# Exponent and high half head by head, low half of head 1 in the next pair, residual as float32 transposes scaled on GpSimd

## The reference

```python
xn = rms_norm(x, g_norm) * (1.0 + scale) + shift        # scale, shift from cond @ W_emb + b_emb
q, k, v = split_heads(xn @ W_qkv)                       # 16 heads of 64
q, k = rms_norm(q, g_q), rms_norm(k, g_k)
attn = softmax(q @ k.T * 64 ** -0.5)
o = attn @ v
x = x + (o + o @ W_out)
x = x + (conv(x, w) + b)                                # depthwise, four taps, causal
```

## Time and profile before

| | |
|---|---|
| median of 3 runs (lowest, highest) | 2456.92 us (2450.82, 2458.89) |
| profiled execution: its own time | 2456.85 us |
| its span on the core | 2454.9 us |
| TensorE matmul / VectorE / ScalarE / GpSimd busy | 95% / 84% / 73% / 26% |
| DMA queue 1, share of 16 engines | 93.4% |
| chain that ended last, by engine | PE 72%, DVE 11%, SyncE's queue 4%, issue 3% |

### The profile page before, as it was taken

One profiled execution on the slowest core, in us unless ns is written; L12 is line 12 of the kernel. 1 busy time (PEld: TensorE's weight loads), 2 busy tenths in 40 slices (PEclk: granted clock), 3 DMA queues, 4 the chain that ended last, 5 costly groups with the idle time before them and its releaser, 6 DMA issues.

```text
span 2454.9 us, 53605 instructions
## 1 busy us (share of the span) xinstructions
PE 2337.2 (95%) x20666; PEld 1529.3 (62%) x20666; DVE 2061.2 (84%) x3239; ACT 1797.1 (73%) x2706; POOL 648.6 (26%) x451
## 2 busy tenths in 40 slices
PE   5799898988899999999999999999999999999899
PEld 0455555555466666666666666666666666666688
DVE  7768988888878898888888888888888888888876
ACT  5467788788777777777777787777777777777732
POOL 1122333333333222323322223233212222222100
PEclk9899999999999999999999999999999999999999
DMA  8989989899999999999999999999988998889971
GB/s 361 315 208 230 194 177 200 180 189 225 202 207 181 203 183 215 182 200 231 204 208 191 213 183 201 192 189 222 208 177 172 182 175 162 177 162 176 186 187 52
DMA packets 1234732, 484.94 MB, mean 198 GB/s; under 512 B 1139632, under 2 KB 1197872, under 8 KB 1232048
## 3 DMA queue, kind: packets, MB, share of 16 engines
q1 hardware_dynamic: 1234480, 481.53, 93.4%
HBM read 137.20 MB, written 56.66 MB: 79 GB/s over the span
## 4 chain that ended last, share of the span: by engine, by line
PE 72%; DVE 11%; SPq 4%; issue 3%; ACT 2%; DMA 2%; POOL 1%; ACTq 0%; POOLq 0%
PE proj L1002 32%; PE proj L1036 12%; PE scores L946 11%; PE values L965 11%; DVE p_pair L1540 4%; DVE neg L1531 4%; SPq L750 3%; PE proj L1042 2%; PE values L978 1%; ACT p_pair L1195 1%; DMA w_sb<-w_dram 1%; PE misc L1054 1%; PE misc L1014 1%; PE proj L1014 1%; SPq L706 1%
## 5 line engine op out<-in xcount | busy, mean ns | idle before, releaser
L1002 PE MATMUL proj<-w_sb,xn_sb 128*128 128x384 f16 x6144 | 1034.1, 327 | 26.4 <-DMA w_sb<-w_dram 18.2
L1002 PEld LDWEIGHTS proj<-w_sb,xn_sb 128*128 128x128 f16 x6144 | 592.8, 98 | 431.3 <-issue 50.4
L1187 ACT ACTIVATE late<-scores,bias,l_scale 128x1024 f32<-128x1024 f32 x512 | 615.9, 1204 | 332.6 <-DVE bias L1534 313.7
L1540 DVE TENSOR_TENSOR p_pair<-late,p_pair 128x1024 f16<-128x1024 f32 x512 | 616.4, 1245 | 173.5 <-ACT p_pair L1195 173.2
L1531 DVE TENSOR_REDUCE neg<-scores 128x1 f32<-128x1024 f32 x512 | 623.2, 1217 | 101.7 <-PE scores L946 98.7
L1195 ACT ACTIVATE p_pair<-late 128x1024 f16<-128x1024 f32 x512 | 510.0, 1046 | 0.0
L965 PE MATMUL values<-pT,v_pair 128*64 128x256 f16 x6144 | 385.3, 275 | 13.2 <-ACT inv_all L1255 13.2
L946 PE MATMUL scores<-late 64*128 64x512 f16 x3072 | 376.1, 378 | 18.1 <-ACT late L1187 17.6
L965 PEld LDWEIGHTS values<-pT,v_pair 128*64 128x64 f16 x6144 | 316.4, 110 | 91.8 <-issue 70.1
L1447 POOL TENSOR_TENSOR rs<-ms,power 128x16 f32<-128x16 f32 x63 | 183.1, 2906 | 400.2 <-DVE ms L1554 399.9
L1036 PE MATMUL proj<-late,wo 128*128 128x256 f16 x2304 | 267.5, 273 | 0.8 <-DMA late<-in_x 0.8
(11 more groups left out here) (178 smaller groups left out, 1939.2 us busy)
## 6 DMA issues: line engine op xcount, KB each, us to landing
w_sb<-w_dram SPq DMA_DIRECT2D x121, 384.0 KB, 4.1
o_dram<-oT_pair SPq DMA_DIRECT2D x124, 128.0 KB, 2.4
out<-late SPq DMA_DIRECT2D x54, 256.0 KB, 2.9
x_in<-in_x SPq DMA_DIRECT2D x25, 512.0 KB, 4.8
late<-in_x SPq DMA_DIRECT2D x25, 512.0 KB, 4.2
wq_raw<-in_L_cond_W_qkv SPq DMA_DIRECT2D x8, 1536.0 KB, 10.7
late<-o_dram SPq DMA_DIRECT2D x12, 1024.0 KB, 6.3
xn_dram<-late SPq DMA_DIRECT2D x21, 512.0 KB, 3.3
```

The lines of the kernel that those rows point to most:

```text
L1002: last = nc.tensor.matmul(proj[:, t % 2, 0:6 * DH], xn_sb[:, t, i * K + c, :], w_sb[:, c, j, :], start=(c == 0 and i == j == 0), stop=(c = ...
L1187: nc.scalar.activation(prob[:, h, :], scores[:, h, :], ACT.Exp, bias=bias[:, s:s + 1], scale=const["l_scale"][:, 0:1], accum_out=total[:, ...
L1540: nc.vector.tensor_tensor(p_pair[:, s % 4, 1, :], prob[:, h, :], p_pair[:, s % 4, 0, :], ALU.subtract).then_inc(lo_done, 1)
```

## The change

The diff does three things. ScalarE's list has exponent and high half of head 0 and then those of head 1, instead of both exponents and then both high halves. VectorE's list has the low half of head 1 behind the first maximum of the next pair, instead of at the end of its own pair. The residual's `x` block is scaled in its place by `x_residual` on GpSimd, and added by two transposes against the plain identity (`is_transpose=True`) instead of two products with the scaled identity; `set_scale`, `scaled_eye` and their semaphores go, and `read_y` takes its scale from the table `y_scale`.

```diff
@@ TensorE, out_product (add_x alike)
                 for a in range(2 if c0 == 0 else 0):
                     last = nc.tensor.matmul(dst[:, a * P:(a + 1) * P], xr_[:, a, (2 * hh + i) * P:(2 * hh + i + 1) * P],
-                                            eye_x[:], start=False, stop=(a == 1))
+                                            const["eye32"][:], start=False, stop=(a == 1), is_transpose=True)
@@ TensorE, unit
-                        free0 = ((oT_ld, 8 * (T - par) + 16), (xr_ld, 16 * (T + 1)), (eye_done, T - par + 2),
+                        free0 = ((oT_ld, 8 * (T - par) + 16), (xr_up, T + 1),
                                  (qkv_ev, K * w + 7) if qkv else (y_ev, 2 * T - 1))
@@ ScalarE
-            def scaled_eye(T):
-                act.wait_ge(y_set, T + 2)
-                need(act, op_mm, 2 * T)
-                nc.scalar.activation(eye_x[:], const["eye32"][:], ACT.Copy,
-                                     scale=y_now[:, 1:2]).then_inc(eye_done, 2)
@@ ScalarE, read_y
-                                     scale=y_now[:, 0:1]).then_inc(y_ev, 1)
+                                     scale=const["y_scale"][:, T:T + 1]).then_inc(y_ev, 1)
@@ ScalarE, unit
-                    exponent(u, p, 0, par)
-                    exponent(u, p, 1, par)
-                    high(u, p, 0)
-                    high(u, p, 1)
+                    for h in range(2):
+                        exponent(u, p, h, par)
+                        high(u, p, h)
@@ GpSimd
+            def x_residual(T):
+                i = T - (U - K - 1)
+                pool.wait_ge(*((xr_ld, 16 * (T + 1)) if i < 0 else (last_xr_ld[i], 16)))
+                block_ = xr[:] if i < 0 else last_xr[i]
+                nc.gpsimd.tensor_scalar(block_, block_, const["back"][:, T:T + 1], 1.0, ALU.mult,
+                                        ALU.mult).then_inc(xr_up, 1)
@@ GpSimd, unit
+                    if last and p in (0, 2, 4):
+                        x_residual(T + p // 2)
...
+                    if p == 3 and outs and not last:
+                        x_residual(T)
@@ VectorE, unit
                     maximum(u, p, 0)
+                    if p:
+                        low(u, p - 1, 1)
+                    elif begun:
+                        low(u - 1, K - 1, 1)
                     maximum(u, p, 1)
...
-                        if outs and par == 0:
-                            set_scale(T)
...
                     low(u, p, 0)
-                    low(u, p, 1)
```

More of the change, by code:

```diff
@@ L497, in main @@
         oT_pair = sb("oT_pair", [P, 2, QG], F16)
-        eye_x = sb("eye_x", [P, P], F32)
-        one = sb("one", [P, 1], F32)
-        y_now = sb("y_now", [P, 2], F32)
         ends = sb("ends", [P, K, H], F32)
@@ L594, in main @@
         y_first = sem("y_first")
-        one_done = sem("one_done")
-        y_set = sem("y_set")
-        eye_done = sem("eye_done")
+        xr_up = sem("xr_up")
+        ends_set = sem("ends_set")
         op_mm = sem("op_mm")
@@ L1023, in add_x @@
                         nc.tensor.matmul(proj[:, hh, i * QG + a * P:i * QG + (a + 1) * P],
-                                         xr_[:, a, (2 * hh + i) * P:(2 * hh + i + 1) * P], eye_x[:],
-                                         start=False, stop=False)
+                                         xr_[:, a, (2 * hh + i) * P:(2 * hh + i + 1) * P], const["eye32"][:],
+                                         start=False, stop=False, is_transpose=True)
             def out_product(T, par, hh, i, oT_, xr_, free, c0=0, c1=K):
@@ L1294, in read_last_y @@
                 nc.scalar.activation(yT_of(T)[:, 2 + i, H:H + QG], (proj[:, 1, 0:QG], last_y)[i], ACT.Copy,
-                                     scale=y_now[:, 0:1]).then_inc((y_first, y_ev)[i], 1)
+                                     scale=const["y_scale"][:, T:T + 1]).then_inc((y_first, y_ev)[i], 1)
             def read_out(T, hh):
@@ L1378, in unit @@
                         high_values(w, 1 - par, 1)
-                    if last and p == 5:
-                        scaled_eye(U - K)
             for v in range(K):
@@ L1476, in o_lower @@
                 nc.gpsimd.tensor_tensor(o_half(u, g, 1), oT[:], o_half(u, g, 0), ALU.subtract).then_inc(o_low, 1)
+            def x_residual(T):
[4 more added lines that the diff above has]
+                                        ALU.mult).then_inc(xr_up, 1)
             def unit(u, par, qkv, xs, outs, fins):
-                w, v = u + 1, u + K
+                w, v, T = u + 1, u + K, u - K
                 begun = not (static(u) and u == 0)
+                last = u + 1 == U
                 for p in range(K):
+                    if last and p in (0, 2, 4):
+                        x_residual(T + p // 2)
                     if p == 0 and xs:
@@ L1521, in _ @@
             in_units(unit, pool)
-            for g in range(2, 4):
-                o_lower(U - 1, g)
+            o_lower(U - 1, 2)
+            for T in range(U - K + 2, U - K + 4):
+                x_residual(T)
+            o_lower(U - 1, 3)
+            for T in range(U - K + 4, U):
+                x_residual(T)
         @block.vector
@@ L1652, in scale_values @@
                 nc.vector.tensor_tensor(oT[:], values[:, 0:QG], inv_all[:], ALU.mult).then_inc(o_done, 1)
-            def set_scale(T):
-                need(dve, y_ev, 2 * T)
-                need(dve, eye_done, T)
-                for i, name in enumerate(("y_scale", "back")):
-                    nc.vector.tensor_scalar(y_now[:, i:i + 1], one[:], const[name][:, bass.ds(T, 1)], None,
-                                            ALU.mult).then_inc(y_set, 1)
             def convolve(T, par, hh, i):
@@ L1719, in unit @@
                         normalise(w, 1)
-                    if last and p == 5:
-                        set_scale(U - K)
                     if u in (1, 2) and p < 4:
@@ L1745, in unit @@
                         normalise(w, 1)
-            nc.vector.memset(ends[:], 0.0)
-            nc.vector.memset(one[:], 1.0).then_inc(one_done, 1)
-            dve.wait_ge(one_done, 1)
+            nc.vector.memset(ends[:], 0.0).then_inc(ends_set, 1)
+            dve.wait_ge(ends_set, 1)
             for v in range(K):
@@ L1804, in _ @@
             in_units(unit, dve)
+            low(U - 1, K - 1, 1)
             invert(U - 1, 3, 1)
```

33 lines of the change are left out of this document (14 added, 19 removed).

## The result

The changed kernel takes 2562.24 us (median of 4 runs, 2554.7 to 2565.72); the kernel before took 2454.83 us beside it. The ratio is 1.042 (95% interval 1.0398 to 1.0443). The forecast was 2485 us with a range of 2448 to 2504: the sign is right, the size is not, and the time lies outside the range. The profiled execution has a span of 2558.8 us.

The account below looks back on a forecast made before the run. TensorE and the softmax loop were taken to bound steady units together, the loop the last unit, TensorE the tail. Steady units +32, early units +3, last unit and tail -7 gave +28 on 2456.85: 2485 us, range 2448 to 2504.

Parts of the forecast that it names:

- What bounds: In steady units TensorE and the softmax loop arrive together at pair 7's end; in the last unit the loop bounds.
- the tail and the last unit: Tail -6.4 us, last unit's pairs 4 to 7 -2.2 us, against 2 us for block 23; together -7.
- The early units: Units before unit 8: about +3 us, from +0.5 x 7 and the loop's small gains.
- its slipping weight load: In early units the next weights' load, after GpSimd's pieces, can slip by a port meeting: +0.5 x 7.
- Part 1: Residual on TensorE: two transposes save 0.23 us a group, 0.92 us a steady unit, wholly eaten there by the loop.
- Part 2: GpSimd's scaling of a 128x1024 block: 2 us, bounds 1.1 and 2.8, hidden in steady units.
- Block 23: Output block whose load TensorE already waits 0.77 us for; its scaling adds 2 us, up to 2.8, once.
- Part 3, the replay: Steady unit stepped from pair 5: low half between maxima makes 6.88 us between scores; unit 0.75 us longer.
- Part 4, the port: VectorE's low half meets GpSimd's in pair 6: 1.13 us if GpSimd is first, otherwise 0.5; lower price taken.
- The 0.15 for pair 5: Price in us of a similar port meeting in pair 5, counted as costing 0 to 0.5.
- the three that were faster: TensorE bounds throughout: 2427, chance 0.12; loop without late power or port meeting: 2453, 0.13; loop with late power: 2466, 0.2.
- The upper end of the forecast: 2504 us: GpSimd first at the port, steady units 2.05 us longer, 47 + 4 - 7.

Follow-up runs that it names:

- the run with the pause: Changed kernel with GpSimd's pair 6 pieces behind VectorE's low half, two unused VectorE multiplications before pair 5's low half, and 5 idle-time matmuls before pair 7's scores: 2495.16 us.
- the kernel with GpSimd's pieces later: Changed kernel, but in pair 6 GpSimd begins head 1's half for pair 5 only after VectorE's low half: 2527.74 us, ratio 1.0294.
- the fastest kernel here: Residual change with VectorE's old order, ScalarE's new order only in units 0 to 7 and the last, block 23 loaded three pairs earlier: 2442.54 us, ratio 0.9945.

## Why the prediction was wrong in size, by its steps

**What bounds.** Right: in steady units TensorE and the loop arrive together, and the tail and the last unit gain: -7.8 against -7. The early units are +5.0 against +3, and that they are so near is luck: with VectorE's order alone they are +13.0, with ScalarE's alone -6.4, each in one trace. The forecast had neither, and no run tests its slipping weight load.

**Part 1.** The size is right: 0.22 us a group, and two instructions of the length of a float32 transpose. That a steady unit keeps nothing of it is right too, and the residual part alone showed it.

**Part 2.** The scaling takes 1.11 us on average, the lower bound, where I took 2; 1.97 where it meets VectorE's low halves, in the residual part alone. That it is hidden in steady units was right. Block 23 was mis-sized both ways, for 2 us: in the changed kernel its load is issued 2.3 us ahead of the last unit, and TensorE waits 0.85 us in its place, against 0.77 before; in the residual part alone it is issued 0.45 us ahead, and TensorE waits 4.13 us and has 2.5 of slow matmuls behind that. The scaling takes 1.12 us in both: the rest is the load.

**Part 3, the replay.** Its steps were right to 0.03 us wherever its assumptions held, as the run with the pause shows. Two sentences failed. "Power on GpSimd 1.56 later at 6.98, done 9.88" took the power's 2.90 us from a row in which VectorE's low half began after it; in the new order the low half begins before it, and it takes 3.81. The whole replay sat on that one row, and I moved an instruction ahead of the very thing that the row described. The pause gave it back: 0.73 to 0.90 us a unit. And "pair 7 takes the larger of 6.88 and 6.93" assumes TensorE at its full clock. After 3.47 us of waiting, pair 7's work takes 8.39 to 8.55 us in units 9 to 30 but one (9.49 in unit 23): 1.5 to 1.6 us a unit, the largest term, and absent from the sum.

**Part 4, the port.** The mechanism and the place were right, and of the two ends the dearer came: GpSimd is first, by 0.04 us, in the unit shown, and VectorE's low half takes 2.19 to 2.20 in the others too. Measured 0.99 us a unit by moving GpSimd's pieces, where I counted 0.5. The 0.15 for pair 5 was for the wrong partner: the pieces there cost VectorE 0.06, the power costs 0.9.

The sum of a steady unit, by the runs: what is left of the change without the other three 1.06 (71.76 to 70.70), delayed power 0.90 (72.66 to 71.76), clock 1.44 (74.10 to 72.66), meeting 0.99 (75.09 to 74.10), together 4.39. The forecast had 0.75, 0, 0 and 0.65. Of the 1.06, 0.90 are pairs 5 to 7 (24.31 us from 2095.01 on, before 23.41): 0.72, where the replay had 0.75, and the 0.18 that GpSimd's moved pieces cost in pair 7, which are this experiment's and not the change's. The clock's share of the changed kernel is 0.18 larger for it, 1.62. The other 0.17 is pair 1 (9.66 instead of 9.49), which the forecast left with TensorE; it comes with VectorE's order (9.66 with that alone, 9.49 with ScalarE's or the residual alone), and why is open.

**Rivals.** None of the three that were faster came. The upper end of the forecast, 2504, is 2501 by its own terms (2457 + 47 + 4 - 7). What came was the forecast's mechanism plus a fall of the clock, which was no rival. The replay held the hint: scores of pair 7 at 17.22, less TensorE's 9.76 + 5.78 of work in pairs 5 and 6, is a wait of 1.7 us, and with the two missing terms over 3, but the text never asked how fast TensorE is behind it.

What stays open: why the same wait of 2.48 us is followed by the lower clock in some units and not in others. The length of the wait alone doesn't decide it. The 3.47 us of the changed kernel were followed by it in each of units 9 to 30, 2.35 us with VectorE's order alone in all but one, and 1.98 us (for weights, unit 15 of the changed kernel) and 2.01 us (last unit, ScalarE's order alone) once each; 2.06 us in the last unit of the residual part alone was not, nor was 3.84 us in that of the kernel with GpSimd's pieces later. The kernel before has no wait above 1.87 us from unit 8 on, and none is followed by it. The second thing open is what makes TensorE wait longer for weights in some of the kernels.

## What to carry to other kernels

When a replay moves an instruction, every duration that it takes from a row has to be asked what ran beside it in that row, and in which order the two began. When the sum puts a wait of some microseconds ahead of TensorE in a repeated unit, add the work behind it at the lower clock to the sum, as an upper end at least. And an order that is good where the loop binds can be bad where TensorE binds: switch it by stage, as the fastest kernel here does with ScalarE's order.

## What the runs showed of the hardware

- GpSimd's power, a 128x16 operation of 2.90 us, took 3.81 when a VectorE subtraction of two SBUF inputs had begun 0.18 us before it, and 2.90 or 3.08 when the same subtraction began 0.23 to 0.29 us after it; the 0.9 us are about what the subtraction had left to run. SBUF — State Buffer (the Trainium skill), section Who interferes with whom, has the two engines exclude each other on a shared port, the first for its whole instruction. The trace agrees where the subtraction is first; where the power is first it differs: the subtraction beside it keeps its own 1.21 us (1.24 beside a power of 3.08).
- TensorE's granted clock was 0.61 in the 4 us behind a wait of 3.47 us and 1.00 after them (unit 18 of the changed kernel); behind waits of 2.24 to 2.65 us it was kept in part of the units. 5 matmuls (1.1 us) in the wait ahead of pair 7's scores kept it there in all of units 8 to 30, and 14 cost more than they saved once the wait was shorter. TensorE: Matmul & The Clock Gate (the Trainium skill), section Part 1: The HAM clock gate, says that the clock follows how busy the engine has been, with levels of 1.2 and 2.4 GHz; the trace agrees (0.61 is a mean over both).
- A 128x1024 float32 multiplication by one number per partition takes GpSimd 1.12 us when VectorE leaves it alone, 2.08 in most units of the residual part alone, where VectorE's low halves run beside it, against 2.13 us (mean in the changed kernel) for the subtraction of the same size.
